# Adaptive-layernorm block with a selective scan and a tree feed-forward: one exponential of each group goes to another PSUM bank, three steps' work order changes

## The reference, cut to what matters

```
# branch 1: selective state-space layer (256 inner channels, 16 states)
u     = silu(causal_conv4(h @ W_in[:, :256]) + conv_b)
z     = h @ W_in[:, 256:]
dt_r, B, C = split(u @ W_xp)                       # 8, 16, 16 columns
delta = softplus(dt_r @ W_dt + dt_bias)
state[e, n] = exp(delta[e] * A[e, n]) * state[e, n] + delta[e] * B[n] * u[e]     # over time
y[e]  = sum_n state[e, n] * C[n] + D[e] * u[e]
x     = x + ga * ((y * silu(z)) @ W_out)
# branch 2: soft binary tree, depth 8, 256 leaves
gate  = sigmoid((h2 @ Wq.T) @ routers.T)
x     = x + gb * ((product of gates along each path) @ leaf_values @ Wout.T + b)
```

## Time and profile before

| | us |
|---|---|
| median of 3 runs | 488.3 (487.87 to 488.62) |
| the profiled execution | 486.38 |
| its span, first to last instruction | 484.6 |
| DVE busy | 447.3 (92%) |
| POOL busy | 422.1 (87%) |
| PE busy | 397.5 (82%) |
| ACT busy | 378.3 (78%) |
| mean granted clock of TensorE | 0.961 |

### The profile page before, as it was taken

How to read it: one execution, slowest core, us unless ns; L and a number is a source line. 1 busy time by engine, 2 the same in 40 slices (tenths; PEclk the granted TensorE clock), 3 DMA queues, 4 the chain that set the end, 5 groups by cost and what they waited for, 6 DMA issues and landing times. The chain is left out here.

```text
span 484.6 us, 6708 instructions
## 1 busy us (share of the span) xinstructions
PE 397.5 (82%) x2133; PEld 272.7 (56%) x2164; DVE 447.3 (92%) x539; ACT 378.3 (78%) x690; POOL 422.1 (87%) x236
## 2 busy tenths in 40 slices
PE   6979775996679887997799888997789787588596
PEld 2546454673547545674557546674657555566374
DVE  6598999989999999999999899989999899999872
ACT  4377985688877998788967998699966997777825
POOL 6149899999999989999899889999999889999910
PEclk8899987999799999999989999999999998799999
DMA  6675027200722018300733018300732027300001
GB/s 160 169 257 206 0 76 299 89 0 1 283 96 83 1 45 331 110 0 2 252 133 99 2 52 323 108 2 0 265 127 93 0 62 313 109 2 22 0 1 43
DMA packets 24146, 51.06 MB, mean 105 GB/s; under 512 B 4521, under 2 KB 14256, under 8 KB 20016
## 3 DMA queue, kind: packets, MB, share of 16 engines
q1 hardware_dynamic: 24112, 50.64, 30.5%
HBM read 48.01 MB, written 2.62 MB: 104 GB/s over the span
## 5 line engine op out<-in xcount | busy, mean ns | idle before, releaser
L606 POOL TENSOR_TENSOR hc<-h,c_rows 128x1024 f32<-128x1024 f32 x127 | 297.8, 2363 | 21.3 <-DVE h L1382 20.8
L1382 DVE TENSOR_TENSOR_SCAN h<-dA,state,dbu 128x512 f32<-128x512 f32 x192 | 233.5, 1263 | 7.3 <-ACT dA L697 7.3
L697 ACT ACTIVATE dA<-delta,a_neg 128x512 f32<-128x512 f32 x256 | 172.8, 685 | 39.6 <-DVE h L1382 39.1
L1123 PE MATMUL yb<-ident,hc 128*128 128x128 f32 x1024 | 151.1, 282 | 20.1 <-POOL hc L606 18.9
L1123 PEld LDWEIGHTS yb<-ident,hc 128*128 128x128 f32 x1024 | 127.6, 146 | 65.7 <-issue 41.0
L1395 DVE TENSOR_TENSOR dbu<-du,bb 128x1024 f32<-128x1024 f32 x88 | 105.3, 1197 | 4.3 <-remote 2.0
L593 POOL TENSOR_TENSOR dbu<-du,b_rows 128x1024 f32<-128x1024 f32 x40 | 94.5, 2363 | 4.5 <-DMA b_rows<-bc_dram 4.5
L1382 DVE TENSOR_TENSOR_SCAN h<-dA,dbu 128x512 f32<-128x512 f32 x64 | 74.0, 1203 | 2.8 <-ACT dA L697 2.6
L1023 PE MATMUL mf<-f_hT,w_conv 128*128 128x512 f32 x112 | 53.3, 599 | 2.0 <-ACT zu L757 1.4
L1148 PE MATMUL bb<-b_parts,sel 128*128 128x512 bf16 x63 | 25.1, 398 | 30.9 <-DVE dbu L1395 29.6
L1148 PEld LDWEIGHTS bb<-b_parts,sel 128*128 128x128 bf16 x88 | 8.7, 99 | 47.4 <-DVE dbu L1395 27.3
(11 more groups left out here) (206 smaller groups left out, 512.2 us busy)
## 6 DMA issues: line engine op xcount, KB each, us to landing
c_rows<-bc_dram SPq DMA_DIRECT2D x32, 1024.0 KB, 7.7
b_rows<-bc_dram SPq DMA_DIRECT2D x40, 256.0 KB, 8.7
xs<-in_L_attn_x_dram SPq DMA_DIRECT2D x8, 256.0 KB, 3.7
out_dram<-xs SPq DMA_DIRECT2D x7, 256.0 KB, 5.6
ygT<-in_L_attn_conv_w_dram SPq DMA_DIRECT2D x2, 256.0 KB, 4.2
bc_dram<-xd SPq DMA_DIRECT2D x8, 64.0 KB, 1.6
w_in<-in_L_attn_W_in_dram SPq DMA_DIRECT2D x2, 128.0 KB, 4.0
probT<-in_L_wmod_dram SPq DMA_DIRECT2D x1, 256.0 KB, 4.0
```

Of the source, the lines that this page charges most:

```text
L606: nc.gpsimd.tensor_tensor(hc[:, pair % RC, :, :], h[:, pair % RH, :, :], c_rows[:, q, n % NQ, :].unsqueeze(1).broadcast_to([P, HALVES, T]) ...
L697: nc.scalar.activation(dA[ke % RD][:, :], delta[:, ge % 2, half, :], ACT.Exp, scale=a_neg[:, half, n:n + 1]).then_inc(s_dA, 1)
L1123: last = nc.tensor.matmul(bank[:, tile], hc[:, pair % RC, half, tile], ident[:, :], start=False, stop=n == N - 1, is_transpose=True, skip_ ...
L1382: v.tensor_tensor_scan(h[:, pair % RH, half, :], dA[k % RD][:, :], dbu[:, pair % RW, half, :], start, ALU.mult, ALU.add).then_inc(s_scan, 1)
```

## The change

A constant `SPARE` = 13 names one step of each group. The exponential of that step is written into the front's product bank instead of `dA[k % 3]`, and the scan of that step reads it there. ACT issues it one step sooner, at step 10 behind the exponential of step 12 and ahead of the Silu block; step 11 then has no exponential. It waits for ACT's own read of z half 1 (in the last group for an event that is long past) and no longer for a scan. Delta's half 0 moves from PE's steps 11 and 12 to 14 and 15, and its first piece waits for the scan of step 13.

```diff
-              ("dt", 0): (1, (11, 12)), ("xd", 0): (1, (18, 19)), ("tr", 0): (2, (28,))},
+              ("dt", 0): (1, (14, 15)), ("xd", 0): (1, (18, 19)), ("tr", 0): (2, (28,))},
...
+    SPARE = F_SILU + AHEAD_EXP + 1
...
+        def dA_bank(k):
+
+            return mb["f"][0] if k % STEPS == SPARE else dA[k % RD]
...
-                    ke = k + AHEAD_EXP
-                    if 0 <= ke < K:
+                    ahead = [k + AHEAD_EXP]
+                    if s == F_SILU:
+                        ahead = [k + AHEAD_EXP, k + AHEAD_EXP + 1]
+                    elif s == F_SILU + 1:
+                        ahead = []
+                    for ke in ahead:
+                        if not 0 <= ke < K:
+                            continue
                         ge, se = divmod(ke, STEPS)
                         n, half = divmod(se, HALVES)
                         if se < HALVES:
                             wait_delta(act, ge, se)
-                        if ke >= RD:
+                        if ke % STEPS == SPARE:
+                            if front:
+                                wait_read(act, "f", "z", 1, f)
+                            else:
+                                act.wait_ge(s_lo, GROUPS)
+                        elif ke >= RD:
                             act.wait_ge(s_scan, ke - RD + 1)
...
-                        nc.scalar.activation(dA[ke % RD][:, :], delta[:, ge % 2, half, :], ACT.Exp,
+                        nc.scalar.activation(dA_bank(ke)[:, :], delta[:, ge % 2, half, :], ACT.Exp,
                                              scale=a_neg[:, half, n:n + 1]).then_inc(s_dA, 1)
...
                     if piece == 0:
                         pe.wait_ge(s_silu, g + 1)
+                        if side == "f":
+                            pe.wait_ge(s_scan, (g - 1) * STEPS + SPARE + 1)
                         if (side, g) == ("t", 1):
                             pe.wait_ge(s_wtake, 1)
...
-                        v.tensor_tensor_scan(h[:, pair % RH, half, :], dA[k % RD][:, :], dbu[:, pair % RW, half, :],
+                        v.tensor_tensor_scan(h[:, pair % RH, half, :], dA_bank(k)[:, :], dbu[:, pair % RW, half, :],
```

## The result

| | before | changed |
|---|---|---|
| median of 5 runs, us | 488.19 (486.69 to 488.62) | 491.74 (491.08 to 494.73) |
| span of the profiled execution, us | 484.6 | 490.4 |
| mean granted clock of TensorE | 0.961 | 0.948 |

The ratio is 1.0088, 95% interval 1.0065 to 1.0111. By the ratio the kernel became slower by 0.9%, 4.3 us (the means of the five runs; the medians alone differ by 3.6), where 1.1 us were forecast. The time lies in the stated range and on the stated side, but at the second rival's 491.6 and not at the forecast's 489.4. So a wait read from these two traces shows where time goes, and the runs say how much it is worth.

A forecast was written before the change was run, and what follows sets the result against it. DVE was taken as the bound. Profiled execution 486.38 us + 1.6 (group 0) - 0.5 (groups 1 to 6) = 487.5; the same +1.1 on the 488.3 median gave 489.4 us, range 487.4 to 491.8.

The forecast's parts named there:

- stated range: Whole kernel: measured time expected between 487.4 and 491.8 us.
- stated side: Whole kernel: slower, given 0.50, against 0.38 for same and 0.12 for faster.
- second rival: Groups 1 to 6: PE's clock also falls in two groups, about 1.1 us each, giving 491.6 us; chance 0.22.
- What bounds the kernel, and the target: DVE bounds, busy 447.3 of 484.6 us; its waits for exponentials total 9.9 us, 6.1 of them at scan 13.
- The exponential gains next to nothing: Groups 1 to 6: the wait moves to step 14, 1.45 us in group 5; about 0.5 us won in all.
- Delta's product and the order of PE's queue: Fill of pair 9 queues 0.86 us later: hidden in groups 1 to 6; group 0's dbu 0.47 us late.
- The Softplus at step 17: ACT in group 5: delta's second piece ends by about 331, read some 332.2, so hidden with about a microsecond to spare.
- The clock in group 0: PE idles about 4.8 us, then half clock adds 1.5 us; dbu of pair 9 2.0 late, net +1.6.
- POOL's slack: Group 0, hc of pair 9: 0.4 us of slack absorbs part of the 2.0 us delay, leaving 1.6.
- The clock in groups 1 to 6: PE idles 2.2 us in one piece; forecast kept full clock, with the fill hidden by 0.6 us.
- rival 2: Groups 1 to 6: half clock in two of six groups makes DVE wait about 1.1 us each; 491.6 us, chance 0.22.

The follow-up runs named there:

- e2: Kernel before with only the exponential of step 13 moved ahead of the Silu block, in its usual bank; ratio to the kernel before 1.0013.
- e4: e2 plus ACT's read of out moved from step 11 to 12, behind the exponential of step 14; ratio to the kernel before 0.9963.
- e3: Changed kernel plus four unread matmuls on PE at steps 11 and 12, filling the idle stretch; ratio to the kernel before 0.9991.
- both further profiles: Two more profiles of the changed kernel, nothing altered; single runs of 494.83 and 492.17 us.
- e1: Kernel before with only delta's half 0 moved to steps 14 and 15; ratio to the kernel before 1.0089.
- e5: Changed kernel plus the unread matmuls at steps 11 and 12 in groups 1 to 6 only; ratio to the kernel before 1.0036.
- e8: e7 plus unread bf16 matmuls ahead of the early fill, 12 in group 0, 7 in groups 1 to 6; ratio to the kernel before 0.9965.
- e6: Changed kernel with PE's fill of pair 9 at step 13 instead of 15, ahead of delta's products; ratio to the kernel before 1.0012.
- e7: e6 plus exponentials of steps 13 and 14 ahead of the Silu block, ordinary banks re-rotated, read of out a step later; ratio to the kernel before 1.0213.

## Why the prediction was wrong

**What bounds the kernel, and the target.** Right. The waits at scan 13 were the target, and they are gone: none in groups 0 to 6. One reading was wrong, without effect on the sum: of the seven other waits for an exponential only five stand behind a Softplus block. The two largest, 0.84 and 1.42 us at 420.20 and 458.44, stand behind the block of the tree's gates (lines 801 to 803).

**The exponential gains next to nothing.** Right, and shown by e2: the wait moves to step 14, with 1.44 us measured and 1.45 forecast in group 5. The sum of these gains, 0.5 us, is below what e2 could measure. The prediction took the wait at step 14 to consist of the Silu block and the read of out behind it; e4 shows the read's part, 0.49 us.

**Delta's product and the order of PE's queue.** Right, with dbu of pair 9 0.47 us late as worked out. Half 0 in front of the fill takes its 0.86 us in group 0 and is hidden in the others at full clock (e3, and group 4 of the changed kernel). The Softplus at step 17, which was to be in time, is so only at full clock: in the changed kernel ACT waits there for delta's product, 2.82 us in group 0 and 0.30 in each of groups 1, 2, 3 and 5. DVE had no wait behind it, being held by the fill already.

**The clock in group 0.** The mechanism was right, the term was mis-sized. I took half of the 3.1 us of work at half clock, 1.5, for a dbu 2.0 us late. The profile has it 3.26 late, near my upper end of 3.6, and both further profiles agree within 0.2 us; only e1's own profile came out near the middle. POOL's slack was about as worked out, 0.3 us for 0.4: 2.95 and 2.93 us stay, against 1.6 forecast. By runs (e5 against e3) it is some 2.2 us, from which 1.6 is not told apart.

**The clock in groups 1 to 6.** This is the step that failed. The forecast had these groups at full clock and put the falls into the second rival, with a chance of 0.22 and two groups at 1.1 us. The profile shows four, each with a wait of 1.03, and the second and third profile five and four. The price of one was right, 1.1 for 1.03; how often it falls due was not. By runs (the changed kernel against e5) they cost 2.5 us together. I had compared the new idle stretch of 2.2 us with the one of 2.81 that ended at half clock, and taken the difference, and denser neighbours, as safety. The 2.02 us measured were enough in most groups.
**The number.** That the median stands at rival 2's 491.6 is partly luck. Rival 2 adds two falls at 1.1 us to a group 0 of 1.6. The profile has four falls at 1.03 and 2.9 us left of group 0, which is more; the runs have 2.5 and 2.2 us, each within 1.5 either way.

**What stays open.** Why groups 4 and mostly 6 keep the clock behind the same idle stretch was not found. That the change makes the waits for fills by way of the clock is shown by e3 and e5, and that unread work holds the clock also by e8; how much of the 2.5 us would be left if only the fill's place were mended, at the slow clock, is not known, since e6 took the falls away too.

## What to carry to other kernels

Work on an engine off the critical path may be what keeps that engine's clock up: before moving it, look at what idle stretch it leaves and who is served first behind that stretch. When a wait for a queue is removed, read what else the queue does before the next item of the same kind; here a read of 0.5 us decided between nothing (1.0013) and 0.4% (0.9963). A bank or buffer is worth adding only if the place it frees is the one that is waited for: the move of the exponential needed none.

## What the runs showed of the hardware that was not expected

Idle stretches of TensorE of 2.02 us, with work on both sides, were followed by half clock in most groups of the changed kernel (4, 5 and 4 of 6 in its three profiles; 2 of 6 in e1's), at once or up to a microsecond later, and by full clock in others with the same instructions (granted 0.58 and 1.00 in the windows above). In e6, where 1.62 us of idle were left, none of groups 1 to 6 had it (1.50 in group 3). In group 0, behind an idle stretch of the same 4.64 us, the slow clock held beyond 61.3 in the changed kernel's profile (half 0 took 1.91 us, half 1 after it 1.71), and in e1's it was over for the same two (1.14 and 1.02). Adding matmuls whose results nobody reads made a kernel faster twice: 0.97% from the changed kernel to e3 by their ratios, 2.5% from e7 to e8.
